# Moving the rotation of queries and keys ahead of the sum with the 257th key in VectorE's queue (layer 0 attentions)

## What is computed

```python
x = x + _L0_xattn_ref(_layernorm(x), ctx_1024, 32, ...)   # single head, 32 largest of 257 scores kept
x = x + _L0_attn_ref(_layernorm(x), W_Q, W_K, W_V, W_O)   # 16 heads of 8, rotary positions
...
# cross attention
scores = einsum('btd,bsd->bts', q, k) * scale
vals, idx = top_k(scores, 32)            # the others become -inf
attn = softmax(masked scores); ctx = einsum('bts,bsd->btd', attn, v); return ctx @ Wo.T + bo
# self attention
q = q * cos + rotate_half(q) * sin;  k = k * cos + rotate_half(k) * sin
attn = softmax(q k / sqrt(8));  return (attn v) @ W_O
```

## Time and profile before

| | |
|---|---|
| median of 3 runs | 1757.32 us (1751.78 to 1759.29) |
| profiled execution, its own time | 1745.2 us |
| its span in the trace | 1743.4 us |
| mean granted clock of TensorE | 0.951 of full speed |
| busy: PE / PEld / DVE / ACT / POOL | 86% / 66% / 62% / 49% / 31% of the span |

### The profile page before, as it was taken

One profiled execution on the slowest core, in us unless ns is written; L12 is line 12 of the kernel. 1 busy time (PEld: TensorE's weight loads), 2 busy tenths in 40 slices (PEclk: granted clock), 3 DMA queues, 4 the chain that ended last, 5 costly groups with the idle time before them and its releaser, 6 DMA issues. The chain is left out here.

```text
span 1743.4 us, 46044 instructions
## 1 busy us (share of the span) xinstructions
PE 1503.6 (86%) x15538; PEld 1144.6 (66%) x15538; DVE 1078.3 (62%) x3384; ACT 853.5 (49%) x2372; POOL 534.5 (31%) x1140
## 2 busy tenths in 40 slices
PE   3887888757689669999999999969999999499998
PEld 2666666546467446666666666657777777488887
DVE  3888888846300247778777877746666666433333
ACT  2455555521232247777777777734444443244443
POOL 1344444410710624444444444422222222000000
PEclk9999999965889869999999999989999999799999
DMA  5444633200111111111111111000000000000000
GB/s 183 148 154 154 213 117 102 79 1 2 50 56 46 44 41 34 33 33 33 33 33 33 33 33 34 21 1 0 0 0 0 0 0 0 1 7 12 6 12 12
DMA packets 62703, 78.31 MB, mean 45 GB/s; under 512 B 7736, under 2 KB 50244, under 8 KB 62528
## 3 DMA queue, kind: packets, MB, share of 16 engines
q1 hardware_dynamic: 60608, 74.12, 14.0%
q0 software_dynamic: 2048, 3.58, 0.7%
HBM read 69.51 MB, written 8.78 MB: 45 GB/s over the span
## 5 line engine op out<-in xcount | busy, mean ns | idle before, releaser
L1607 ACT ACTIVATE c_pr<-c_pS,c_nm 128x257 f32<-128x257 f32 x512 | 238.2, 471 | 97.6 <-DVE c_nm L1741 97.6
L1741 DVE TENSOR_REDUCE c_nm<-c_pS 128x1 f32<-128x257 f32 (+1 forms) x384 | 173.3, 506 | 42.4 <-PE c_pS L1487 42.1
L1981 ACT ACTIVATE s_k<-s_pK 128x512 f32<-128x512 f32 x128 | 76.4, 597 | 177.0 <-PE s_pK L1908 177.0
L1491 PE MATMUL c_pT<-cst,c_pr 128*128 128x128 f32 x1024 | 162.8, 284 | 0.0
L1361 ACT ACTIVATE f_hid<-f_pH,vec 128x512 f32<-128x512 f32 x128 | 88.0, 687 | 128.2 <-PE f_pH L1323 127.0
L1908 PEld LDWEIGHTS s_pK<-s_hT,AH 128*128 128x128 f32 x1024 | 123.6, 195 | 25.9 <-ACT s_k L1981 22.7
L1383 DVE SCALAR_TENSOR_TENSOR X<-f_pY,f_mk,X 128x128 f32 x256 | 72.1, 344 | 110.4 <-PE f_pY L1333 110.4
L1908 PE MATMUL s_pK<-s_hT,AH 128*128 128x128 f32 x1024 | 137.3, 284 | 0.5 <-ACT s_hT L1976 0.5
L1491 PEld LDWEIGHTS c_pT<-cst,c_pr 128*128 128x128 f32 x1024 | 111.2, 141 | 37.6 <-issue 37.6
L1333 PEld LDWEIGHTS f_pY<-f_w,f_hid 128*128 128x128 f32 x1024 | 122.3, 192 | 5.0
L1333 PE MATMUL f_pY<-f_w,f_hid 128*128 128x128 f32 x1024 | 124.2, 276 | 0.0
(11 more groups left out here) (297 smaller groups left out, 3193.7 us busy)
## 6 DMA issues: line engine op xcount, KB each, us to landing
a_ctxT<-in_ctxT SPq DMA_DIRECT2D x32, 514.0 KB, 3.7
c_ctxT<-in_ctxT SPq DMA_DIRECT2D x128, 128.5 KB, 2.2
a_ctxN<-in_ctxR SPq DMA_DIRECT2D x32, 512.0 KB, 4.0
f_w<-in_f_w SPq DMA_DIRECT2D x16, 256.0 KB, 3.5
rows_in<-a_zero SPq DMA_DIRECT2D x7, 320.0 KB, 4.1
f_h<-rows_in SPq DMA_DIRECT2D x7, 320.0 KB, 3.4
rows_out<-f_y SPq DMA_DIRECT2D x7, 320.0 KB, 2.4
a_ctxL<-in_ctxL SPq DMA_DIRECT2D x128, 16.0 KB, 3.5
```

Of the source, the lines that this page charges most:

```text
L1491: mm = pe.transpose(pT[:, c, j, :], pr[:, b % 2, j, c * P:(c + 1) * P], k("ident"))
L1607: act.activation(pr[:, b % 2, c, :], pS[:, c, 0:S], ACT.Exp, bias=nm[:, c:c + 1], accum_out=den[:, b % 2, c:c + 1]).then_inc(e_ready.sem, 1)
L1741: dve.tensor_reduce(nm[:, c:end], pS[:, c:end, 0:S], AX.X, ALU.max, negate=True).then_inc(max_ready.sem, 1)
```

## The change

VectorE's list of one slot gets a new order. `rotate(a)` goes from behind `sums_with_last(u)` to ahead of it. `largest(2)` goes ahead of `self_inverse_sums(z)`, and `rotated(a)` goes from behind `mark(2)` to behind `self_inverse_sums(z)`. No instruction is added or removed, no other engine's list is touched, and all waits stay those of their steps.

```diff
--- before.py
+++ after.py
@@ -763,14 +763,14 @@
                 run(largest(1), t)
                 run(lambda g: n1.vector_rows(dve, x_of(g)), w_)
                 run(mark(1), t)
+                run(rotate, a)
                 run(lambda u: sums_with_last(u, p, r), u)
-                run(rotate, a)
+                run(largest(2), t)
                 run(self_inverse_sums, z)
-                run(largest(2), t)
+                run(rotated, a)
                 run(self_sums, z)
                 run(lambda g: n1.vector_moments(dve, g), w_)
                 run(mark(2), t)
-                run(rotated, a)
                 run(largest(3), t)
                 run(scale_w, w_)
                 run(add_self_output, z)
```

## The result

The changed kernel takes 1772.8 us (median of 6 runs, 1767.9 to 1776.3) against 1756.6 us (6 runs, 1751.8 to 1760.1): ratio 1.0092, 95% interval 1.0068 to 1.0116. It is slower by 16 us where +5.9 us was forecast, and 1772.8 lies outside the range of 1755 to 1770. In a later series of runs, with before at 1744.8, the same kernel had 1756.1 us: +11.3, ratio 1.0058 (1.0041 to 1.0075).

The account below looks back on a forecast made before the run. The prediction took a 10.26 us loop per slot through TensorE and VectorE to bound the kernel; 27 x 0.205 = 5.5 us plus 0.1 and 0.25 gave +5.9, so 1757.3 + 5.9 = 1763 us, range 1755 to 1770.

Parts of the forecast that it names:

- The loop, and the delay on it: Attention slots: a 10.26 us loop through TensorE and VectorE; the rotation ahead of L687 delays it 0.205 us in the mean.
- Behind L687: VectorE from L687 to L739: moments and scale_w about as early as before; the gap ahead of L739 grows, unusable.
- rotated earlier: qk comes 0.9 us earlier, worth nothing; rstd falls from 0.79 to 0.55 us without gain; last slots lose 0.25 us.
- transfers: The next load of summed context waits for cs, 0.2 us later in a slot of over 10: costs nothing.
- The sum: Whole kernel: 27 x 0.205 = 5.5 us, some 0.1 and 0.25 us more, together +5.9 us.
- rival 4: TensorE's clock falls to 1.2 GHz in three more slots, 4.4 us on top of 5.9: 1768 us, chance 0.06.
- Rivals 1 to 3: 1: GpSimd's norm chain paces slot, 1751 us (0.05); 2: delay absorbed, 1757 us (0.11); 3: full price, 1768 us (0.12).
- rival 3: Full price: no overlap around the rotation, L687 0.375 us later per slot, 10.5 us in all, 1768 us, chance 0.12.

Follow-up runs that it names:

- d1: Kernel before, order unchanged, plus one VectorE instruction (0.60 us) between the second mark and the sum with the 257th key: +16.3 us, ratio 1.0082.
- e2: Changed kernel with the rotation put back behind the sum with the 257th key, the rest of the change kept: +0.5 us against before, ratio 1.0002.
- e3: Changed kernel with three extra unread matmuls per slot on TensorE, two behind self_scores, one behind turn_z: +6.5 us against before, ratio 1.0038.
- a2: The changed kernel once more, in a later series: +11.3 us against before, ratio 1.0058.
- e5: Changed kernel with two extra matmuls per slot on TensorE ahead of turn_sums, where it waits for u: +10.8 us against before, ratio 1.0060.
- b2: b1 with three extra unread matmuls per slot on TensorE: +17.6 us against before, ratio 1.0107.
- b5: b4 with three extra unread matmuls per slot on TensorE: -0.9 us against before, ratio 0.9995.
- b1: Kernel before with the fourth mark moved ahead of scale_w: 1815.0 us, +70.2 us against before, ratio 1.0399.
- b4: Kernel before with the fourth mark directly behind scale_w and ahead of the addition L739: +9.2 us against before, ratio 1.0060.

## Why the prediction failed

- *The loop, and the delay on it*: right. L687 0.93 us behind the second mark, 3.49 us on to L739, 4.00 us on to the logits copy; slots of 10.42 to 10.51 us against the forecast 10.44 to 10.51. Confirmed from outside by d1.
- *Behind L687; rotated earlier; transfers*: right, as far as a steady slot shows. rstd 0.55 us, scale_w early, nothing gained (e2: +0.5 us). The wait ahead of L739 0.69 us (forecast 0.5 to 0.7).
- *The sum*: its terms hold. With the clock up they come to 6.5 us measured (e3) for 5.9 worked out. But the sum has all slots at the upper clock level. That is the step that failed: the prediction put three or more falls in rival 4 with a chance of 0.06, with "240 us at the upper level with gaps of the same kind in each slot" as the reason. So the sum had the clock at nothing. The pauses of the thin stretch were of the same size (busy 2.49 of 4.00 us against 2.55 of 3.99), only the wait for u was longer, and the clock fell all the same; in the two profiles of the changed kernel it did four and six times between 75 and 350 us. The price of one was right: 1.45 us from the one slot seen before, 1.2 in the mean of the first profile's four long slots (4.9 in all) and 1.4 in a2's six (8.4). With these the profiles place 9.6 us in the attentions in the first series and 11.7 in a2; where the rest of the first series' 16.2 lies is open.
- *Rivals 1 to 3*: none. A steady slot neither lost nor gained more than the sum says. The +11.3 us of the second series lies near rival 3's 10.5 and rival 4's 10.3 alike, so the total alone could not have told them apart.
- *A reading of the rows*: the prediction has the 17.3 us ahead of L687 released by TensorE; the earlier trace rows give it 9.4 of them, and 7.9 to "issue", time in which the profile shows nothing that was waited for. The sum doesn't use the 17.3.
- What stays open: why a slot longer by 0.06 or 0.2 us lets the clock fall where 10.27 us doesn't. The mean busy share alone is not it (e5), the order is not it (d1), the pause ahead of u is not needed for it (e5). With three matmuls more in the thin stretch the falls are gone (e3, b2, b5). Whether the length of the slot acts by itself, or where its pauses then come to lie, was not isolated; d1 only shows that a delay suffices.

## What to carry to other kernels

An idle time directly ahead of an instruction is no room for others if that instruction is on the loop: look who waits for it next, and subtract the queue time of what you put there from the gap (0.60 us into 0.36 to 0.43 us of gap made every slot 0.2 us longer). Where TensorE's work is thin for part of each period, price a longer period with and without the granted clock, and test a reordering with some filler matmuls in the thin part: that tells the order's own cost (6.5 us) from the clock's (5 to 10 here, 52 in b1). And before an instruction is pushed back on VectorE, see what GpSimd starts at that moment.

## What the hardware showed that was not expected

- With a slot of 10.33 us instead of 10.27 (b4) the clock fell three times to 1.2 GHz between 75 and 350 us; at 10.92 us, unfilled (b1), its mean in the stretch was 0.80. With e3's fillers all of them stayed at 1.00 (b5, b2). Whether the slot's length or the order that makes it does this was not isolated.
- A higher mean busy share of TensorE didn't keep the clock up: TensorE was busy 193.6 of 240 us at a clock of 1.00 in before, 201.0 at 0.99 in e5.
- VectorE's `tensor_scalar` of 128x128 took 0.39 us when it started 0.26 us ahead of GpSimd's 1.03 us instruction, and 1.02 us when it started 0.09 us behind.
